# Another PSUM bank for one mask, an earlier load, and a reordered gate stage in a two-branch AdaLN block

## The chip, the cores and the metric

The kernel runs on one core of a Trainium2 chip, in one launch. The metric is device time in microseconds, the median of repeated runs. The engines are TensorE (PE), VectorE (DVE), ScalarE (ACT), GpSimd (POOL) and SyncE (SP), which issues nearly all of the DMAs.

## The reference

`x` has 2 batches of 512 rows of 512 features (`b`, `s`, `d`). A conditioning vector gives six modulation rows per batch. Two branches follow each other, each with a layernorm, a modulation and a gated residual:

```python
mod = (_silu(L0_c) @ L0_wmod).reshape(L0_c.shape[0], 6, 1, -1)
sa, ca, ga, sb, cb, gb = (mod[:, 0], mod[:, 1], mod[:, 2], mod[:, 3], mod[:, 4], mod[:, 5])
ga = (2 * (ga >= 0) - 1) * jnp.maximum(jnp.abs(ga), 0.25)   # gb alike
h = _layernorm(x, axis=-1) * (1 + ca) + sa
x = x + ga * _L0_attn_ref(h, mask, weight, bias)
h = _layernorm(x, axis=-1) * (1 + cb) + sb
x = x + gb * _L0_ffn_ref(h, w1, w3, w2, lora_A1, lora_B1, ...)
```

The first branch is one matmul with a 512 x 512 weight whose 32 x 32 blocks are kept where the sum of an integer mask over the block is above zero, plus a bias. The second is a gated feed-forward (512 to 1376 and back) with a rank-16 addition to each of its three weights. All is float32.

## The kernel before, in words

**Tiling.** Rows lie in eight tiles of 128 (batch 0: tiles 0 to 3, batch 1: 4 to 7; `b, t = divmod(n, T)`), features in `KT` = 4 groups of 128 (`k`). Float32 products are made of three float32r matmuls: each operand is split into a rounded high part and a low part (`ht_hi`/`ht_lo`, `wa_hi`/`wa_lo`), and high x high, high x low and low x high are summed in PSUM; these are `m` = 0, 1, 2 of `attend(b, k, m)` (L1093). Where the code has `b` in a modulation's index, it is the batch.

**Order.** Nothing plans the work. Each engine has one list of steps written by hand (SP from L357, POOL from L469, ACT from L622, DVE from L848, PE from L1175) and runs it in order; between engines there are only semaphores. So a step that waits holds up everything that stands behind it in its engine's list, also what is ready.

**The masked weight**, once per `k`: DVE's `mask_sum(k)` (L756) adds the mask in rows of 32; PE's `mask_blocks(k)` (L1073) adds over 32 partitions into a corner of `mask_bank(k)`, bank `side[0]` for k = 0, 1 and `acc[1]` for k = 2, 3 (for those it waits for `h_done(1)`, as `acc[1]` holds the second transposed group); DVE's `mask_on(k)` (L762) makes the flags and `mask_weight(k)` (L768, instruction L773) multiplies the weight in place; ACT's `masked_weight_high(k)` (L620) and POOL's `masked_weight_low(k)` (L467) split it.

**The normalised input**, once per batch: DVE's `moment(n)` (L699, L701), POOL's `root(n, 2)` for two tiles (L403, L406), DVE's `centres` (L717), then ACT's `norm` (L549) or DVE's `norm` (L710). PE's `turn(q)` (L978, L999) transposes one feature group of four tiles. Its banks are `acc[k]` for batch 0 and `acc[TURN_BANKS[k]]`, in the order 1, 0, 2, 3, for batch 1; q = 8 to 11 are the second branch's groups of batch 0. ACT's `high(q)` (L566) modulates and rounds, `whole(q)` (ACT L575 or DVE L736) modulates without rounding, and `low(q)` (POOL L419, some by DVE L725) is the difference. The first modulation's columns come from `mod_products` (L1026) and `first_columns`.

**The attention's accumulators.** Batch 0 sums in `front` = `up_a`, `up_b`, `side[0]`, `side[1]`, batch 1 in `acc`. `attend_bias(b)` (L1091) opens the four sums with the bias, one matmul for each, on four different groups of 32 rows.

**The gate.** `gate_rows(0)` (L1055) makes the raw gate, ACT's `gate_size(0)` its absolute value, DVE's `gates_of(0)` (L779, L782) the clamped gate in `gates_a`, and signals `gates_ready`. PE's `gate_spread` (L1068) broadcasts it over 128 partitions with eight float32 matmuls of 32 rows (16 records), two to each of the four `acc` banks, batch outside and bank inside, with one signal after the last; DVE's `gate_copy(q)` (L790) brings it to SBUF, once per bank, into the space of the mask. `turn(4 + k)` waits for copy k + 1. With the copies `attn_gate(n)` (L813) multiplies each attention tile, and `add_x1(n)` (DVE L818 for batch 0, POOL L437 for batch 1, by `X1_POOL`) adds it to `x`. The moments of the second branch follow.

**The rest.** `lora_high(n)` (ACT L616) and `lora_part(n)` (DVE L797) split the six pieces of the low-rank factors; POOL's `spread(j)` (L430) and PE's `merge(r)` (L1137, L1141) form their products, DVE's `merge` (L827) adds them to the weights streamed in from L378 on, `weight_low` (L833) makes `w_lo`. From about 53 us on PE works through `up` (L1156) and `down` (L1169 to L1171) for 2 x 11 hidden groups.

The DVE list from the last mask to the residual is the part that the change reorders most:

```python
            mask_on(3)
            mask_weight(3)
            moment(4)   # ... moment(5), moment(6), moment(7)
            centres(T)
            gates_of(0)
            norm(T + 2)
            norm(T + 3)
            for q in TURN_BANKS:
                gate_copy(q)
            lora_part(0)
            whole(4)    # ... whole(5), whole(6), whole(7)
            attn_gate(0)   # ... to attn_gate(3), then add_x1(0) to add_x1(3)
```

## Time and profile before

| | |
|---|---|
| median of 3 runs (lowest to highest) | 252.25 us (252.08 to 252.29) |
| the profiled execution: its own time, its span | 252.32 us, 250.5 us |
| PE busy | 242.3 us, 97% |
| DVE, ACT, POOL busy | 135.9, 89.6, 97.3 us |
| granted TensorE clock, mean | 1.000 |
| HBM read, written | 21.18 MB, 2.10 MB |

How to read it: the span runs from the first to the last instruction; the time is a little longer, by what lies around the program. A timeline row gives start, duration, engine, source line, operation, and how many instructions it joins. Where an instruction begins before the one ahead of it on the same engine has ended, the two overlap in the engine's pipeline. Idle time before an instruction and what released it stand in brackets.

### The profile page before, as it was taken

The numbers are of one execution on the slowest core, as the hardware profiler recorded it, in microseconds if no ns is written. First come the engines' busy times: TensorE is split into PE (matmuls) and PEld (weight loads), VectorE is DVE, ScalarE is ACT, GpSimd is POOL, SyncE is SP. The second block draws the span as 40 slices with busy tenths as digits, with TensorE's granted clock in tenths as the row PEclk, the third lists the DMA queues.
The fourth block names the chain that finished last, engine by engine and source line by source line (L and its number), as shares of the span: only waits on it lengthen the run. The fifth ranks groups of instructions, "written<-read, shape, count | busy, mean of one in ns | idle before, by whom it ended". The sixth has DMA issues, their size and how long they took to land.

```text
span 250.5 us, 3526 instructions
## 1 busy us (share of the span) xinstructions
PE 242.3 (97%) x1265; PEld 192.8 (77%) x1265; DVE 135.9 (54%) x221; ACT 89.6 (36%) x151; POOL 97.3 (39%) x102
## 2 busy tenths in 40 slices
PE   7799999899999999999999999999999999999993
PEld 6677768787788888888888778888888888888772
DVE  2847899899999744744754631741233123312224
ACT  2376554843324465465422311122112221222110
POOL 1377492326532131230210351497346435643300
PEclk9999999999999999999999999999999999999999
DMA  6999991023224413213217520030000000000005
GB/s 184 345 384 407 413 401 42 3 84 119 51 84 127 126 47 123 84 42 128 84 46 107 45 13 0 38 132 0 0 0 4 0 0 0 4 0 0 0 0 169
DMA packets 13041, 24.02 MB, mean 96 GB/s; under 512 B 1240, under 2 KB 2648, under 8 KB 13024
## 3 DMA queue, kind: packets, MB, share of 16 engines
q1 hardware_dynamic: 12864, 23.65, 30.2%
q8 instruction: 10, 0.16, 0.3%
q10 hardware_dynamic: 160, 0.15, 0.2%
q14 instruction: 7, 0.06, 0.1%
HBM read 21.18 MB, written 2.10 MB: 93 GB/s over the span
## 4 chain that ended last, share of the span: by engine, by line
PE 82%; DVE 6%; DMA 3%; issue 3%; POOL 2%; ACT 1%; SPq 1%; DVEq 0%; POOLq 0%; ACTq 0%
PE up_b L1156 25%; PE up_a L1156 24%; PE acc L1170 8%; PE acc L1171 8%; PE acc L1169 8%; DMA wmod_sb<-in_wmod 3%; PE side L1137 2%; DVE xt L839 1%; DVE stats L699 1%; PE acc L999 1%; DVE wa L813 1%; PE side L1141 1%; DVE xt L818 1%; PE acc L1106 1%; POOL ht_lo L419 1%
## 5 line engine op out<-in xcount | busy, mean ns | idle before, releaser
L940 DVE TENSOR_TENSOR g<-up_b,g 128x512 f32<-128x512 f32 (+1 forms) x22 | 15.2, 690 | 64.5 <-PE up_b L1156 64.5
L1170 PE MATMUL acc<-w_lo,g_hi 128*128 128x512 f32 (+1 forms) x88 | 34.7, 394 | 0.0
L1171 PE MATMUL acc<-w_hi,g_lo 128*128 128x512 f32 (+1 forms) x88 | 34.7, 394 | 0.0
L1169 PE MATMUL acc<-w_hi,g_hi 128*128 128x512 f32 (+1 forms) x88 | 34.6, 394 | 0.0
L670 ACT ACTIVATE g<-up_a 128x512 f32<-128x512 f32 (+1 forms) x22 | 13.1, 597 | 58.8 <-PE up_a L1156 58.5
L827 DVE SCALAR_TENSOR_TENSOR raw<-side,raw 128x512 f32<-128x512 f32 (+2 forms) x33 | 21.5, 676 | 22.3 <-PE side L1137 15.7
L677 ACT ACTIVATE g_hi<-g 128x512 fp32r<-128x512 f32 (+1 forms) x22 | 13.9, 633 | 49.4 <-DVE g L940 49.4
L462 POOL TENSOR_TENSOR w_lo<-work,w_hi 128x512 fp32r<-128x512 f32 (+1 forms) x11 | 14.2, 1287 | 41.1 <-ACT w_hi L604 41.1
L597 ACT ACTIVATE w_hi<-raw 128x512 fp32r<-128x512 f32 (+2 forms) x33 | 20.3, 626 | 21.2 <-DVE raw L827 21.1
L944 DVE TENSOR_TENSOR g_lo<-g,g_hi 128x512 fp32r<-128x512 f32 (+1 forms) x22 | 22.9, 1041 | 8.7 <-ACT g_hi L677 8.4
L1156 PE MATMUL up_a<-ht_hi,w_lo 128*128 128x512 f32 (+1 forms) x88 | 24.2, 396 | 0.4 <-DVE w_lo L833 0.4
L1156 PE MATMUL up_a<-ht_hi,w_hi 128*128 128x512 f32 (+1 forms) x88 | 24.3, 397 | 0.0
L833 DVE TENSOR_TENSOR w_lo<-raw,w_hi 128x512 fp32r<-128x512 f32 (+2 forms) x33 | 23.3, 736 | 1.6
L1156 PE MATMUL up_b<-ht_hi,w_lo 128*128 128x512 f32 (+1 forms) x88 | 24.1, 395 | 0.0
L1156 PE MATMUL up_b<-ht_hi,w_hi 128*128 128x512 f32 (+1 forms) x88 | 24.0, 394 | 0.0
L1156 PE MATMUL up_a<-ht_lo,w_hi 128*128 128x512 f32 (+1 forms) x88 | 24.0, 394 | 0.0
L1156 PE MATMUL up_b<-ht_lo,w_hi 128*128 128x512 f32 (+1 forms) x88 | 24.0, 394 | 0.0
L430 POOL TENSOR_SCALAR b<-parts,half_on 128x128 fp32r<-128x128 f32 (+1 forms) x22 | 14.2, 658 | 18.0 <-PE side L1137 15.0
L454 POOL TENSOR_TENSOR work<-w_hi,w_lo 128x512 f32<-128x512 f32 (+1 forms) x11 | 15.0, 1359 | 13.5 <-DMA work<-gates_f 12.1
L1156 PEld LDWEIGHTS up_a<-ht_hi,w_lo 128*128 128x128 f32 (+1 forms) x88 | 16.2, 186 | 5.0 <-DVE w_lo L833 0.9
L1171 PEld LDWEIGHTS acc<-w_hi,g_lo 128*128 128x128 f32 (+1 forms) x88 | 16.5, 188 | 3.9
L1156 PEld LDWEIGHTS up_a<-ht_lo,w_hi 128*128 128x128 f32 (+1 forms) x88 | 16.3, 185 | 4.2
(172 smaller groups left out, 379.3 us busy)
## 6 DMA issues: line engine op xcount, KB each, us to landing
raw<-in_ffn SPq DMA_DIRECT2D x33, 256.0 KB, 2.7
wmod_sb<-in_wmod SPq DMA_DIRECT2D x4, 1024.0 KB, 11.5
xt<-in_x SPq DMA_DIRECT2D x8, 256.0 KB, 8.2
wmod_sb<-in_wmod SPq DMA_DIRECT2D x1, 2048.0 KB, 15.1
out<-xt SPq DMA_DIRECT2D x8, 256.0 KB, 2.7
mask_sb<-in_mask SPq DMA_DIRECT2D x4, 256.0 KB, 9.2
wa<-in_weight SPq DMA_DIRECT2D x4, 256.0 KB, 9.2
lora_raw<-in_lora SPq DMA_DIRECT2D x1, 512.0 KB, 10.4
```

Source lines behind the costliest of these rows:

```text
L430: nc.gpsimd.tensor_scalar(b13[:, n, 0:w], f32(parts[:, LORA_B13 + j * P:LORA_B13 + j * P + w]), half_on[:, n:n + 1], None, ALU.mult).then_ ...
L454: nc.gpsimd.tensor_tensor(dst, f32(down_hi[j][0:w]), f32(down_lo[j][0:w]), ALU.add).then_inc(down_summed, 1)
L462: nc.gpsimd.tensor_tensor(down_lo[j][0:w], gated_sum[j % 2][0:w], f32(down_hi[j][0:w]), ALU.subtract).then_inc(gated_low_ready, 1)
L597: nc.scalar.activation(dst, src, ACT.Copy).then_inc(w_high_ready, 1)
L827: nc.vector.scalar_tensor_tensor(w, merge_bank(r)[0:rows, 0:cols], SCALING, w, ALU.mult, ALU.add).then_inc(merged, 1)
L833: nc.vector.tensor_tensor(low_part, src, f32(high), ALU.subtract).then_inc(w_ready, 1)
L940: nc.vector.tensor_tensor(g[0:w], up_b[0:w], g[0:w], ALU.mult).then_inc(g_ready, 1)
L944: nc.vector.tensor_tensor(g_lo[s % 2][0:w], g[0:w], f32(g_hi[s % 2][0:w]), ALU.subtract).then_inc(g_low_ready, 1)
L1156: last = nc.tensor.matmul(dst[0:w], w_part[j][:, k, n], h[b][:, k], start=(m == 0 and k == 0), stop=(m == 2 and k == KT - 1))
L1169: nc.tensor.matmul(acc[t][:], hi, down_hi[j][0:w], start=(j == 0), stop=False)
L1170: nc.tensor.matmul(acc[t][:], hi, down_lo[j][0:w], start=False, stop=False)
L1171: last = nc.tensor.matmul(acc[t][:], lo, down_hi[j][0:w], start=False, stop=(j == HT - 1))
```

## The change

It gives `mask_bank(1)` the bank `acc[3]`, so that `attend_bias(0)` can come ahead of `mask_blocks(1)` on PE, and moves `turn(3)`, `mask_blocks(2)` and `mask_blocks(3)` in PE's list. SP issues the four loads of batch 1's `x` ahead of the load of the gate's part of `wmod` (both 1 MB). `gate_spread` goes bank by bank and signals after each; two of the four copies go to ACT (a new semaphore `gate_row_by_act`); it runs after `attend(0, 3, 0)`. DVE and ACT make their norms of batch 1 ahead of `gates_of(0)` and `gate_size(0)`. POOL waits for `gates_ready` ahead of `low(3)` and `masked_weight_low(3)`, which swap places and come after two roots. `lora_part(1)` moves from behind `columns()` to just behind `lora_part(0)`, with `lora_high(1)` ahead of it on ACT. `add_x1(3)` goes to POOL, where it waits for three additions of DVE.

```diff
 
 WHOLE_DVE = (4, 5, 6, 7, 9, 11)
 
-X1_POOL = (4, 5, 6, 7)
+X1_POOL = (3, 4, 5, 6, 7)
 
 TURN_BANKS = (1, 0, 2, 3)
-GATE_COPIES = T
+GATE_COPIES = T // 2
 
 CENTRED = {0: 2, 1: 2, 4: 4, 5: 4, 8: 6, 9: 6, 10: 8}
 NORMS_ACT = (2, 4, 7)
...
         gates_ready = sem("gates_ready")
         spread_out = sem("spread_out")
         gate_row_ready = sem("gate_row_ready")
+        gate_row_by_act = sem("gate_row_by_act")
         gate_row_loaded = [sem(f"gate_row_loaded{b}") for b in range(B)]
         stats_ready = sem("stats_ready")
         moments_ready = sem("moments_ready")
...
             return acc[t] if b else front[t]
 
         def mask_bank(k):
-            return acc[1] if k >= 2 else side[0]
+            return (side[0], acc[3], acc[1], acc[1])[k]
 
         def mod_out_at(second, f):
             if second:
...
             load_first_mod(1)
             load_attention(2)
             load_attention(3)
+            load_x(1)
             load_mod(GATE_A, SHIFT_F, wmod_ga_loaded)
-            load_x(1)
             for n in range(LORA_FIRST):
                 load_lora(n)
             load_mod(SHIFT_F, GATE_F, wmod_f_loaded)
...
             def add_x1(n):
                 b, t = divmod(n, T)
                 pool.wait_ge(attn_gated, n + 1)
+                if n < T:
+
+                    pool.wait_ge(x1_by_dve, n)
                 nc.gpsimd.tensor_tensor(xt[:, b, t], mid[n % T], xt[:, b, t], ALU.add).then_inc(x1_by_pool, 1)
 
             def add_x2(n):
...
             low(1)
             masked_weight_low(2)
             low(2)
-            masked_weight_low(3)
-            low(3)
             root(T, 2)
             root(T + 2, 2)
+
+            pool.wait_ge(gates_ready, 1)
+            low(3)
+            masked_weight_low(3)
             spread(0)
             low(KT)
             low(KT + 1)
             low(KT + 2)
             low(KT + 3)
+            add_x1(T - 1)
             root(2 * T, 2)
             root(2 * T + 2, 2)
             spread(1)
...
                 nc.scalar.activation(gate_abs[:], gate_rows_out(n), ACT.Abs, scale=2.0
                                      ).then_inc(gate_abs_ready, 1)
 
+            def gate_copy(q):
+
+                act.wait_ge(spread_out, TURN_BANKS.index(q) + 1)
+                act.wait_ge(block_on_ready, KT)
+                src = acc[q][:, 2 * P:(2 + B) * P].rearrange("p (b n) -> p b n", b=B)
+                nc.scalar.activation(mask_sb[:, 0:B, q * P:(q + 1) * P].bitcast(F32), src, ACT.Copy
+                                     ).then_inc(gate_row_by_act, 1)
+
             def lora_high(n):
                 lo, hi = LORA_CUTS[n]
                 act.wait_ge(lora_loaded[n], 16)
...
             masked_weight_high(3)
             high(3)
             whole(3)
-            gate_size(0)
             norm(T)
             norm(T + 1)
+            gate_size(0)
             lora_high(0)
+            for q in TURN_BANKS[0::2]:
+                gate_copy(q)
+            lora_high(1)
             high(4)
             high(5)
             high(6)
             high(7)
-            for n in range(1, len(LORA_CUTS)):
+            for n in range(LORA_FIRST, len(LORA_CUTS)):
                 lora_high(n)
             mod_evacuate()
             norm(2 * T)
...
 
             def gate_copy(q):
 
-                dve.wait_ge(spread_out, 1)
+                dve.wait_ge(spread_out, TURN_BANKS.index(q) + 1)
                 dve.wait_ge(block_on_ready, KT)
                 src = acc[q][:, 2 * P:(2 + B) * P].rearrange("p (b n) -> p b n", b=B)
                 nc.vector.tensor_copy(mask_sb[:, 0:B, q * P:(q + 1) * P].bitcast(F32), src
...
                 b, t = divmod(n, T)
                 dve.wait_ge(attn_out, n + 1)
                 dve.wait_ge(gate_row_ready, GATE_COPIES)
+                dve.wait_ge(gate_row_by_act, GATE_COPIES)
                 if b:
 
                     dve.wait_ge(*x1_done(n - T))
...
             mask_weight(2)
             first_columns(1)
             mask_sum(3)
+            moment(4)
             mask_on(3)
             mask_weight(3)
-            moment(4)
             moment(5)
             moment(6)
             moment(7)
             centres(T)
-            gates_of(0)
             norm(T + 2)
             norm(T + 3)
-            for q in TURN_BANKS:
+            gates_of(0)
+            for q in TURN_BANKS[1::2]:
                 gate_copy(q)
             lora_part(0)
+            lora_part(1)
             whole(4)
             whole(5)
             whole(6)
...
             add_x1(0)
             add_x1(1)
             add_x1(2)
-            add_x1(3)
             moment(2 * T)
             moment(2 * T + 1)
             moment(2 * T + 2)
             moment(2 * T + 3)
             centres(2 * T)
             columns()
-            lora_part(1)
             centres(2 * T + 2)
             norm(2 * T + 3)
             gates_of(1)
...
                 pe.wait_ge(normed, NORMS_DVE[i])
                 if i == 1:
 
-                    pe.wait_ge(gate_row_ready, k + 1)
+                    pe.wait_ge(gate_row_ready if k % 2 else gate_row_by_act, k // 2 + 1)
                 elif i == 2 and k == 0:
 
                     pe.wait_ge(attn_gated, T)
...
                 pe.wait_ge(gates_ready, 1)
                 pe.wait_ge(cols_ready, 2)
                 pe.wait_ge(h_ready, KT)
-                for b in range(B):
-                    for q in range(KT):
-                        rows = slice(q * QUAD, (q + 1) * QUAD)
+                for q in TURN_BANKS:
+                    rows = slice(q * QUAD, (q + 1) * QUAD)
+                    for b in range(B):
                         row = q * QUAD + b
                         last = nc.tensor.matmul(acc[q][:, (2 + b) * P:(3 + b) * P],
                                                 ident[rows, row:row + 1].broadcast_to([QUAD, P]), gates_a[rows],
                                                 start=True, stop=True)
-                last.then_inc(spread_out, 1)
+                    last.then_inc(spread_out, 1)
 
             def mask_blocks(k):
                 blocks = slice(k * NB, (k + 1) * NB)
...
                 if b:
 
                     pe.wait_ge(gate_row_ready, GATE_COPIES)
+                    pe.wait_ge(gate_row_by_act, GATE_COPIES)
                 for t in ts:
                     if b:
                         pe.wait_ge(*h_done(KT + TURN_BANKS.index(t)))
...
             turn(1)
             turn(2)
             fill(FILL_H)
-            mask_blocks(1)
             pe.wait_ge(ones_ready, 1)
             pe.wait_ge(bias_ready, 1)
             pe.wait_ge(cols_ready, 1)
+            pe.wait_ge(block_on_ready, 1)
+            attend_bias(0)
+            mask_blocks(1)
+            attend(0, 0, 0)
             pe.wait_ge(block_on_ready, 2)
-            attend_bias(0)
-            attend(0, 0, 0)
+            turn(3)
             mod_products(0, 1)
-            turn(3)
+            attend(0, 0, 1)
             mask_blocks(2)
-            attend(0, 0, 1)
             first_columns(1)
             attend(0, 0, 2)
-            mask_blocks(3)
             attend(0, 1, 0)
             attend(0, 1, 1)
+            mask_blocks(3)
             attend(0, 1, 2)
             attend(0, 2, 0)
-            gate_rows(0)
             attend(0, 2, 1)
             attend(0, 2, 2)
+            gate_rows(0)
+            attend(0, 3, 0)
             gate_spread()
-            attend(0, 3, 0)
             turn(4)
             turn(5)
             turn(6)
```

## Rows read from the trace of the kernel before

**Rows 1.** The page: busy us, share, instructions by engine; GB/s in 40 slices

```profile
PE 242.3 (97%) x1265; PEld 192.8 (77%) x1265; DVE 135.9 (54%) x221; ACT 89.6 (36%) x151; POOL 97.3 (39%) x102
...
GB/s 184 345 384 407 413 401 42 3 84 119 51 84 127 126 47 123 84 42 128 84 46 107 45 13 0 38 132 0 0 0 4 0 0 0 4 0 0 0 0 169
```

**Rows 2.** Waits of PE: waiting, waited for, us in total, times, longest

```profile
PE up_a L1156 <- DVE w_lo L833: 0.4, 1, 0.4
```

**Rows 3.** Timeline, 14 to 18 us, all engines (start us, us)

```profile
14.41 0.29 PE L1080 MATMUL side<-mask_part,const 128*128 128x16 f32 x2
...
14.95 0.69 DVE L773 TENSOR_TENSOR wa<-wa,block_on 128x512 f32<-128x512 f32 x1
...
15.06 0.46 PE L1091 MATMUL up_a<-bias_parts,ones 32*128 32x512 f32 x1 [0.36 <-DVE block_on L765]
...
15.34 1.44 POOL L419 TENSOR_TENSOR ht_lo<-hbuf,ht_hi 128x512 fp32r<-128x512 f32 x1 [0.38 <-ACT hbuf L575]
...
17.01 0.78 ACT L575 ACTIVATE hbuf<-acc,shift,one_plus 128x512 f32<-128x512 f32 x1
```

**Rows 4.** Timeline, 16 to 21 us, all engines

```profile
16.62 1.08 PE L1026 MATMUL acc<-wmod_sb,silu_c 128*32 128x128 f32 x32
...
17.97 1.30 POOL L419 TENSOR_TENSOR ht_lo<-hbuf,ht_hi 128x512 fp32r<-128x512 f32 x1
...
18.67 1.15 DVE L773 TENSOR_TENSOR wa<-wa,block_on 128x512 f32<-128x512 f32 x1
...
19.85 0.63 PE L1106 MATMUL side<-wa_hi,ht_lo 128*128 128x512 f32 x2
...
20.85 0.48 PE L1106 MATMUL up_a<-wa_hi,ht_hi 128*128 128x512 f32 x1
```

**Rows 5.** Timeline, 23 to 30 us, all engines

```profile
23.36 0.69 DVE L699 BATCH_NORM_STATS2 stats<-xt 128x6 f32<-128x512 f32 x1 [0.98 <-DMA xt<-in_x]
...
26.51 0.18 DVE L701 BATCH_NORM_AGGREGATE moments<-stats 128x2 f32<-128x6 f32 x1
...
27.43 0.71 POOL L406 TENSOR_TENSOR rstd<-rstd,exponent 128x2 f32<-128x2 f32 x1
...
27.60 0.29 DVE L782 SCALAR_TENSOR_TENSOR gates_a<-gate_abs,gates_a 128x128 f32<-128x128 f32 x1
...
27.94 0.73 PE L1068 MATMUL acc<-gates_a,const 32*128 32x128 f32 x16
...
28.18 1.00 DVE L710 TENSOR_SCALAR work<-xt,moments,rstd 128x512 f32<-128x512 f32 x2 [0.30 <-POOL rstd L406]
...
29.66 1.94 PE L999 MATMUL acc<-const,work 128*128 128x128 f32 x16
```

**Rows 6.** Timeline, 29 to 34 us, DVE and PE

```profile
29.10 1.41 DVE L790 COPY mask_sb<-acc 128x256 f32<-128x256 f32 x4
...
31.14 1.53 DVE L736 TENSOR_SCALAR hbuf<-acc,one_plus,shift 128x512 f32<-128x512 f32 x2
...
33.40 0.54 PE L1091 MATMUL acc<-bias_parts,ones 32*128 32x512 f32 x3
```

**Rows 7.** Timeline, 34 to 46 us, all engines

```profile
34.03 0.68 DVE L813 TENSOR_TENSOR wa<-up_a,mask_sb 128x512 f32<-128x512 f32 x1
...
36.42 1.48 DVE L818 TENSOR_TENSOR xt<-wa,xt 128x512 f32<-128x512 f32 x1
...
37.82 1.88 DVE L818 TENSOR_TENSOR xt<-wa,xt 128x512 f32<-128x512 f32 x3
...
42.76 0.18 DVE L701 BATCH_NORM_AGGREGATE moments<-stats 128x2 f32<-128x6 f32 x1
...
43.07 0.74 DVE L797 SCALAR_TENSOR_TENSOR parts<-parts,const,lora_raw 128x512 fp32r<-128x512 f32 x1
...
43.11 0.78 POOL L403 TENSOR_SCALAR rstd<-moments 128x2 f32<-128x2 f32 x1 [0.52 <-DVE moments L701]
...
45.92 0.66 PE L999 MATMUL up_a<-const,work 128*128 128x128 f32 x4 [0.65 <-ACT work L549]
```

## The prediction

> **What bounds the kernel now.** I read the engine totals first: PE is busy for 242.3 of 250.5 us [rows 1], so from about 60 us on there is nothing but PE work, and the whole question is when that work begins. Then the list of PE's waits: one that the change can touch is an up product waiting 0.4 us for `w_lo` [rows 2]; two more stand in the timelines, 0.36 us of the first bias matmuls for the second mask's flags [rows 3] and 0.65 us before turn(8) [rows 7]. Together 1.4 us: that is all the PE idle time that a better order could win here, and any new PE wait counts against it in full. Then the timelines of DVE, ACT and POOL from 14 to 46 us, for who releases whom.
>
> One thing must be seen in them first. A DVE instruction with both inputs in SBUF and a POOL instruction of that kind don't run together: whichever starts second waits for the first. mask_weight(2) starts at 18.67 while POOL's low(1) runs from 17.97 to 19.27, and takes 1.15 us; it ends 0.55 after POOL [rows 4]. The same instruction at 14.95, ahead of POOL, takes 0.69, and there POOL's low(0), started at 15.34, takes 1.44: it ends 1.14 after DVE [rows 3]. The first add at 36.42 takes 1.48 while POOL is in low(7), and the next three together 1.88, 0.60 each from start to start; POOL's root at 43.11 takes 0.78 behind lora_part(1) at 43.07 [rows 7]. I call this the lock.
>
> **Step 1: bias ahead of the second mask.** The four bias matmuls (side by side, 0.46 us from 15.06) no longer wait for DVE's flags. They move in front of mask_blocks(1), which began at 14.41, so they start there (up to 0.1 later) and attend(0,0,0) starts at about 15.1 instead of 15.06 + 0.46 = 15.5: 0.4 gained. But the mask's sum is now behind them, at 14.85 to 14.95, and so are its flags and mask_weight(1): 14.95 + 0.44 to 0.54 = 15.39 to 15.50. POOL's low(0) depends on none of this and still starts at 15.34 [rows 3]. So POOL is now first, by 0.05 to 0.15 us, and the lock turns round: mask_weight(1) waits to 15.34 + 1.30 = 16.64 and ends at 16.64 + 0.55 = 17.19, not 15.64. That is 1.55 later, and ACT has its wa_hi, high and whole of k = 1 in a queue behind it: whole(1) ended at 17.01 + 0.78 = 17.79 [rows 3] and now ends at 19.34.
>
> **Step 2: what PE meets next.** attend(0,0,0) 1.1, turn(3) 0.5, mod_products 1.0 (16.62 began the latter before), attend(0,0,1) 1.0: PE is at mask_blocks(2) at about 18.76. It waits there for whole(1), as before, but that is at 19.4: 0.6 us idle. attend(0,1,0) then starts at about 20.7, against 20.85. Before, PE's matmuls of 19.85 were through at 20.3 and some 0.3 us was idle around mask_blocks(3) [rows 4], which now comes later and waits for nothing; that gain and the 0.4 of step 1 are nearly used up. mask_weight(2) and (3) each come 1.3 to 1.5 later than before (again partly behind the lock), mask_weight(3) ending at about 23.9.
>
> **Step 3: second x first.** DVE's first statistic of the second half waited for its x until 23.36 [rows 5]. One MB at the 401 to 413 GB/s of these slices [rows 1] is 2.6 us, so x is there at about 20.8 and the gate's weights, which have the same 1 MB, at about 25.3 instead. Neither is late: DVE is at its first moment at 22.0, PE at gate_rows(0) at 26.6. But three of the four moments are queued behind mask_weight(3). A moment is 0.82 (23.36 to 26.51 + 0.18 = 26.69 for four, with the last aggregate [rows 5]): 23.8 + 3 x 0.82 = 26.3, where they ended at 26.7. root(6) follows and ends at 27.55 (before 27.43 + 0.71 = 28.14 [rows 5]). Gained: 0.6 on the norms.
>
> **Step 4: the gates after the norms.** Before, gates_of(0) ran ahead of DVE's two norms and ended at 27.60 + 0.29 = 27.89, call that G. Now the norms (1.00) come first: 27.6 + 1.0 = 28.6, and gates_of 0.55 behind: G = 29.1, 1.2 later. PE has done attend(0,3,0) meanwhile (about 28.8) and waits 0.35 for the spread at 29.15. The spread ended 0.73 after its start [rows 5]. Its first copy can start 0.8 after G and takes 0.4, so turn(4) starts at G + 1.25 = 30.35: before 29.66. Sharing the copies saves two of four starts, 0.33 each [rows 6], off the last turn only, which does not wait for them.
>
> Here the order of the eight spread matmuls matters. Before, neighbours were in different groups of 32 rows, and the 16 records ended together after 0.73 us, which 16 one after another could not; now the four records of one bank share a group. The bounds: the same 0.7, or one record at a time at the 0.11 of the transposes (1.94 us for 16 [rows 5]), 1.9 us. I take the lower, since the next paragraph shows PE with over a microsecond to spare behind it. The Trainium skill ("TensorE: Matmul & The Clock Gate", Part 3, The mechanism) says that matmuls keep strict program order and overlap only across row groups; by that it would be the upper bound, turn(4) would start at G + 1.95, and the sum would not change as long as whole(6) is the later one.
>
> **Step 5: POOL held to the gates, and two lora parts.** low(3) and wa_lo(3) ran as soon as their inputs stood; they now wait for G. POOL starts 0.17 after its releaser (42.94 to 43.11 [rows 7]), so they run from G + 0.17 to G + 2.70 (1.3 each, the second begun a little before the first ends). DVE gets to lora_part(0) after its two copies, at G + 1.48, 0.07 behind the start of wa_lo(3): the lock again, to G + 2.70, and it ends at G + 3.2, where 0.6 alone would do (384 columns against the 0.74 for 512 of lora_part(1) [rows 7]). lora_part(1), moved here from 43.07, adds 0.67. whole(4) starts at G + 3.7. Before, the four started at 31.14 (G + 3.25) and gave way to attn_gate(0) at 34.03 [rows 7], so 0.72 each. PE's attend_bias(1) started at 33.40, when whole(6) ended (31.14 + 2 x 0.72 + 0.8) [rows 6]: G + 5.5 before, G + 5.95 now, 35.05, 1.65 later than before. PE itself is done with attend_last(0) at about G + 4.9, so 1.05 us idle, and even the serial spread (G + 5.55) fits below it.
>
> **Step 6: three adds.** attn_gate(0) starts at G + 6.6 (before G + 6.15). The add at G + 9.0 again finds POOL's low(7), which shifted along with spread(0) to end at G + 9.9; it ends at G + 10.45, then two more at 0.60, not three, and four moments of 0.81. The last moment ends at G + 14.9 = 44.0; before 42.76 + 0.18 = 42.94, G + 15.05 [rows 7]. POOL's add waits for the third DVE add and has 3.3 us for its 1.3: nothing, and only a root stands behind it, which waits for moments anyway. Without lora_part(1) the last root is not locked out and saves about 0.5: it was held from 43.11 to near 43.81, where lora_part(1) ended [rows 7]. ACT's norm(10) then ends at about 46.6, just ahead of PE: PE, 1.65 late with its own queue, is at turn(8) at 46.95. Before, 45.92 with 0.65 idle [rows 7]. So PE is 1.0 late there, the idle is gone. DVE is 0.8 late into its merges, so the 0.4 wait for `w_lo` [rows 2] shrinks to 0.2 and the end is 0.8 late.
>
> **Sum.** In PE's idle time up to attend_bias(1): new 0.6 (step 2), 0.35 and 0.55 (4), 1.05 (5) = 2.55; removed 0.36 before the bias, 0.3 around mask_blocks(3), and 0.25 in restarts after those waits, which I read off as the rest of the starts' difference: +1.65, as in step 5. After it 0.65 is removed before turn(8) and 0.2 of the `w_lo` wait: 1.65 - 0.85 = +0.8 us. The profiled execution took 252.32 us (span 250.5), the median is 0.07 less; 252.32 + 0.8 = 253.1.
>
> **Rivals.** A difference of 0.2% (0.5 us) is about what a measurement of this kernel can tell from no change.
> - *A, the forecast*, 253.1, chance 0.47. The chain of small leads may be wrong by 0.3 either way; low enough, it falls inside 0.5 us.
> - *B, DVE is first at the first lock.* If the flags come 0.1 earlier than I have them, mask_weight(1) starts before low(0) at 15.34. Then whole(1) ends at 18.2, PE does not wait at mask_blocks(2), and G is 28.3. Steps 5 and 6 still hold: attend_bias(1) at 34.25, turn(8) 0.2 late, end 0.2 late: 252.45. Against it: the lead of low(0) is worked out from starts; for it: it is only 0.05 to 0.15. Chance 0.25.
> - *C, faster.* G at 28.3 as in B, and DVE gets past the lora parts before POOL holds the lock, or is let in between low(3) and wa_lo(3): whole(4) at G + 2.95, since ACT's high(4) is ready at G + 2.9. Then attend_bias(1) is at 33.5, three adds and the free root bring norm(10) a whole microsecond earlier, turn(8) starts at 45.4 with no wait, and the `w_lo` wait shrinks too: 0.7 us faster, 251.55. It decides itself at whole(4): anything before G + 3.2 points here. For it: lora_part(0) misses by 0.07 only. Against: lora_part(1) must also wait for ACT's copies. Chance 0.22.
> - *D, the serial spread decides*: if the lock does not hold DVE but the spread takes 1.9, turns, high(4) to high(7) and attend_last come 0.65 later on top of A's late gates: 253.7. Chance 0.06.
>
> **Numbers.** Slower: D, and 0.44 of A's 0.47: 0.50. Within 0.2%: most of B and the rest: 0.27. Faster: C and a little of B: 0.23. The range runs from C to D with 0.1 either side: 251.5 to 253.8. The cases of both signs hold much of the chance; A's own range is 252.7 to 253.6.
>
> **What would show it.** In the changed profile: mask_weight(1) taking over 1.5 us with low(0) ahead of it (step 1; 0.7 means B); PE idle before mask_blocks(2) with ACT's hbuf as the releaser (2); gates_a finished at 29.1 (4); lora_part(0) over 1 us long and PE idle before the bias of the second half, released by DVE (5); three adds, the last root's first instruction well under 0.78 us, no PE wait before turn(8) (6). The forecast is wrong if gates_a is done by 28.3, or if attend_bias(1) starts before 33.9.

## The result, and the profile after

Interleaved with the kernel before on one chip, the changed kernel took 252.84 us (median of 7, 252.57 to 253.53), the one before 252.13 us (7 runs, 251.82 to 252.34): ratio 1.0031, 95% interval 1.0021 to 1.0040. That is slower by 0.3%, +0.71 us; the forecast was +0.8 (253.1 us).

The profiled execution took 253.53 us, the highest of its seven, so its span (251.7) is 1.2 us above before's; the other six spans are 250.7 to 251.2. 0.70 us of the 1.2 is there when the `w_lo` wait ends, at 61.26 us against 60.56, and still at the last matmul, at 246.93 against 246.23. The other 0.5 arises behind that, in the writing of the output. The medians differ by 0.71, so I don't count it as the change's, though no second trace shows it.

The page and PE's list of waits up to 66 us (waiting, waited for, us in total, times, longest):

```profile
PE 242.9 (96%) x1265; PEld 193.3 (77%) x1265; DVE 135.7 (54%) x218; ACT 90.0 (36%) x153; POOL 98.4 (39%) x103
```

```profile
PE acc L1196 <- DVE ht_lo L705: 1.4, 1, 1.4
PE up_b L1044 <- DMA wmod_sb<-in_wmod: 1.0, 1, 1.0
PE acc L1098 <- ACT hbuf L582: 0.5, 1, 0.5
PE acc L1017 <- ACT mask_sb L625: 0.5, 1, 0.5
PE up_a L1175 <- DVE w_lo L852: 0.4, 1, 0.4
PE acc L1086 <- DVE gates_a L800: 0.3, 1, 0.3
PE acc L1110 <- DVE g L754: 0.2, 1, 0.2
```

The first two rows (at 1.4 and 11.4 us) lie before the change's reach. Three of the next are waits that the forecast announced (0.6, 0.55, 0.35). The `w_lo` wait of [rows 2] is unchanged. The last row looks small and is not, as shown below.

Timeline of the changed kernel, 14 to 31 us, all engines (start us, us; the idle time before a group and its releaser stand in brackets):

```profile
14.46 0.50 PE L1110 MATMUL up_a<-bias_parts,ones 32*128 32x512 f32 x1
...
14.90 0.40 PE L1098 MATMUL acc<-mask_part,const 128*128 128x16 f32 x2
...
15.30 1.28 POOL L420 TENSOR_TENSOR ht_lo<-hbuf,ht_hi 128x512 fp32r<-128x512 f32 x1 [0.42 <-ACT hbuf L582]
15.33 0.17 DVE L783 TENSOR_SCALAR block_on<-acc 128x16 f32<-128x16 f32 x1 [1.27 <-PE acc L1098]
15.54 1.59 DVE L791 TENSOR_TENSOR wa<-wa,block_on 128x512 f32<-128x512 f32 x1
...
18.50 0.78 ACT L582 ACTIVATE hbuf<-acc,shift,one_plus 128x512 f32<-128x512 f32 x1
...
19.42 0.36 PE L1098 MATMUL acc<-mask_part,const 128*128 128x16 f32 x2 [0.53 <-ACT hbuf L582]
...
27.55 1.00 DVE L728 TENSOR_SCALAR work<-xt,moments,rstd 128x512 f32<-128x512 f32 x2 [1.21 <-POOL rstd L407]
...
28.79 0.29 DVE L800 SCALAR_TENSOR_TENSOR gates_a<-gate_abs,gates_a 128x128 f32<-128x128 f32 x1
...
29.14 0.75 PE L1086 MATMUL acc<-gates_a,const 32*128 32x128 f32 x16 [0.33 <-DVE gates_a L800]
...
30.41 1.94 PE L1017 MATMUL acc<-const,work 128*128 128x128 f32 x16 [0.52 <-ACT mask_sb L625]
```

The turned lock is in the third to fifth row: POOL at 15.30, mask_weight(1) at 15.54, 1.59 us long, where [rows 3] had DVE at 14.95 with 0.69. gates_a is done at 29.08 (before 27.89, [rows 5]); turn(4) starts 0.75 late.

The same view, 29 to 47 us:

```profile
30.38 1.29 POOL L471 TENSOR_TENSOR wa_lo<-wa,wa_hi 128x512 fp32r<-128x512 f32 x1
30.61 2.14 DVE L815 SCALAR_TENSOR_TENSOR parts<-parts,const,lora_raw 128x384 fp32r<-128x384 f32 x2
...
32.67 1.52 DVE L754 TENSOR_SCALAR hbuf<-acc,one_plus,shift 128x512 f32<-128x512 f32 x2
...
34.11 0.80 DVE L754 TENSOR_SCALAR g<-acc,one_plus,shift 128x512 f32<-128x512 f32 x1
34.13 0.61 PE L1110 MATMUL acc<-bias_parts,ones 32*128 32x512 f32 x2
...
34.97 0.50 PE L1110 MATMUL acc<-bias_parts,ones 32*128 32x512 f32 x1 [0.22 <-DVE g L754]
...
37.94 2.63 DVE L837 TENSOR_TENSOR xt<-wa,xt 128x512 f32<-128x512 f32 x3
...
40.72 1.29 POOL L441 TENSOR_TENSOR xt<-wa,xt 128x512 f32<-128x512 f32 x1 [1.90 <-DVE xt L837]
...
43.63 0.18 DVE L719 BATCH_NORM_AGGREGATE moments<-stats 128x2 f32<-128x6 f32 x1
...
43.98 0.23 POOL L404 TENSOR_SCALAR rstd<-moments 128x2 f32<-128x2 f32 x1 [0.52 <-DVE moments L719]
...
46.61 0.60 PE L1017 MATMUL up_a<-const,work 128*128 128x128 f32 x4
```

PE reaches the bias of the second half at 34.13, 3.7 us after turn(4), as in the kernel before (29.66 to 33.40, [rows 5, 6]). Two of the first three matmuls run; the third needs whole(6), which DVE ends at 34.11 + 0.80 = 34.91. Before, three ran side by side in 0.54 us. So PE shows 0.22 us idle there and loses 0.8: it is 0.73 late at the first of these matmuls and 1.52 late at the third (34.97 against 33.45). Before turn(8) it wins 0.83 back: the 0.65 wait of [rows 7] is gone and almost 0.2 of restarting with it (a matmul that need not wait starts before the one ahead of it has ended: turn(8) now starts 0.48 us behind the start of merge products that take 0.64). At 46.61 it is 0.69 late, and that is what reaches the end.

### The profile page after: what moved, and what is told of

Same layout as the page of the kernel before. It is cut to its first block, busy times and chain, and to the rows that moved or that the text cites. A ratio compares the mean times of both kernels' runs of the same rounds, so it can differ in the third digit from the quotient of the medians.

```text
span 251.7 us, 3531 instructions
## 1 busy us (share of the span) xinstructions
PE 242.9 (96%) x1265; PEld 193.3 (77%) x1265; DVE 135.7 (54%) x218; ACT 90.0 (36%) x153; POOL 98.4 (39%) x103
## 4 chain that ended last, share of the span: by engine, by line
PE 86%; DVE 5%; DMA 3%; issue 2%; SPq 1%; ACT 1%; POOL 0%; DVEq 0%; POOLq 0%
PE up_b L1175 24%; PE up_a L1175 24%; PE acc L1189 8%; PE acc L1188 8%; PE acc L1190 8%; PE acc L1125 4%; DMA wmod_sb<-in_wmod 3%; PE side L1156 2%; DVE xt L858 1%; PE side L1160 1%; DVE stats L717 1%; PE up_a L1044 1%; PE side L1024 1%; SPq L341 1%; DVE wa L791 1%
## 5 line engine op out<-in xcount | busy, mean ns | idle before, releaser
L1188 PEld LDWEIGHTS acc<-w_hi,g_hi 128*128 128x128 f32 (+1 forms) x88 | 16.5, 188 | 3.9
L1189 PEld LDWEIGHTS acc<-w_lo,g_hi 128*128 128x128 f32 (+1 forms) x88 | 16.5, 188 | 3.9
```

The costliest lines, as they stand in the source:

```text
L1188: nc.tensor.matmul(acc[t][:], hi, down_hi[j][0:w], start=(j == 0), stop=False)
L1189: nc.tensor.matmul(acc[t][:], hi, down_lo[j][0:w], start=False, stop=False)
```

## Experiments

Each kernel is the changed one with the edit shown (b3, b4, c1 and c2 have several), measured beside the kernel before. G is the end of gates_a. All times are from the kernel's own profiled execution, except the ratio. The first product of the modulation starts between 10.8 and 11.7 us in these executions; it waits for its weights' DMA in some of them (until 11.44 in the kernel before, 11.39 in the changed one) and for a mask in others (b4, a3), none of which the edits touch. So single times differ by some tenths for no reason of the edit, and the ratio decides.

| kernel | G | turn(4) | PE's arrival, turn(4) + 3.73 | whole(6) done | third bias | turn(8) | ratio (95%) |
|---|---|---|---|---|---|---|---|
| before | 27.89 | 29.66 | 33.40 | 33.39 | 33.45 | 45.92 | |
| after | 29.08 | 30.41 | 34.14 | 34.91 | 34.97 | 46.61 | 1.0031 (1.0021 to 1.0040) |
| a1 | 29.04 | 30.36 | 34.09 | 34.86 | 34.92 | 46.57 | 1.0031 (1.0020 to 1.0043) |
| a2 | 28.49 | 30.46 | 34.19 | 34.73 | 34.78 | 46.42 | 1.0022 (1.0013 to 1.0032) |
| a3 | 29.48 | 30.81 | 34.54 | 34.64 | 34.69 | 46.75 | 1.0013 (1.0004 to 1.0021) |
| a4 | 30.53 | 31.86 | 35.59 | 35.58 | 35.64 | 47.29 | 1.0099 (1.0074 to 1.0124) |
| b1 | 30.46 | 31.79 | 35.52 | 36.28 | 36.34 | 48.00 | 1.0096 (1.0083 to 1.0108) |
| b2 | 28.75 | 30.08 | 33.81 | 34.58 | 34.63 | 46.62 | 1.0032 (1.0020 to 1.0044) |
| b3 | 28.69 | 30.02 | 33.75 | 34.51 | 34.57 | 46.23 | 1.0027 (1.0011 to 1.0043) |
| b4 | 28.37 | 29.69 | 33.42 | 33.52 | 33.58 | 45.64 | 1.0001 (0.9990 to 1.0013) |
| c1 | 27.66 | 28.98 | 32.71 | 32.82 | 32.88 | 44.97 | 0.9979 (0.9969 to 0.9989) |
| c2 | 27.89 | 29.22 | 32.95 | 32.94 | 33.00 | 45.38 | 0.9978 (0.9967 to 0.9988) |
| c3 | 28.66 | 30.04 | 33.77 | 34.49 | 34.54 | 46.20 | 1.0020 (1.0011 to 1.0028) |

whole(6) done is whole(4)'s start + 2.24 (32.67 to 34.91 in the changed kernel). The third bias matmul starts 0.05 to 0.06 behind the later of the two columns to its left, in every kernel.

### a1: the second mask back ahead of the bias

```
-            attend_bias(0)
             mask_blocks(1)
+            attend_bias(0)
             attend(0, 0, 0)
```

> The changed kernel with mask_blocks(1) put back ahead of attend_bias(0) on PE; all else of the change stays. Lock theory: DVE's mask_weight(1) starts at 14.95, ahead of POOL's low(0) at 15.3, and takes 0.7 us and not 1.6; ACT's whole(1) ends at 17.8 and not 19.3; PE's 0.5 us wait before mask_blocks(2) is gone; gates_a is done at 28.2 to 28.4 instead of 29.1; the time falls by 0.4 to 0.6 us from the changed kernel, to about that of the kernel before. Rival (the early flags buy nothing, the gate stage is set by the late second x, the roots and its own order): gates_a stays within 0.2 us of 29.1 and the time within 0.2 us of the changed kernel's.

The first lock is undone, mask_weight(1) takes 0.69 us again from 14.72, and PE's wait ahead of mask_blocks(2) is gone. Nothing is won: ratio 1.0031, and PE waits 1.2 us for gates_a instead of 0.3. The lock has moved to the third mask (timeline of a1, 20 to 24 us):

```profile
21.96 1.29 POOL L420 TENSOR_TENSOR ht_lo<-hbuf,ht_hi 128x512 fp32r<-128x512 f32 x1 [0.24 <-ACT hbuf L582]
...
22.06 1.74 DVE L791 TENSOR_TENSOR wa<-wa,block_on 128x512 f32<-128x512 f32 x1
```

The three moments behind it end at 26.23 (26.27 in the changed kernel), and G is 29.04. The rival was right: of all the early loss (steps 1 and 2) nothing reaches the end, since G is set by DVE's list.

### a2: the gates back ahead of the norms

```
-            norm(T)
-            norm(T + 1)
             gate_size(0)
+            norm(T)
+            norm(T + 1)
...
-            norm(T + 2)
-            norm(T + 3)
             gates_of(0)
+            norm(T + 2)
+            norm(T + 3)
```

> The changed kernel with the gates back ahead of the norms of batch 1 on DVE and on ACT. Theory: gates_a is done at about 28.7 instead of 29.1, since gate_rows now comes late on PE anyway, but the norms then run into POOL's low(3) and low part of the weight, which start when the gates are ready, and whole(4), which sets PE's bias matmuls, stays within 0.4 us of 32.7: time within 0.3 us of the changed kernel's. Rival (the gates behind the norms are what costs the 0.7 us): whole(4) starts at or before 31.9 and the time falls by 0.5 us or more.

G is 0.6 earlier (0.4, counted from the first product of the modulation), but the norms now fall beside POOL's low(3), which gates_a releases. DVE in a2's timeline, and PE's wait (same columns as above):

```profile
28.41 1.95 DVE L728 TENSOR_SCALAR work<-xt,moments,rstd 128x512 f32<-128x512 f32 x2
```

```profile
PE acc L1017 <- DVE work L728: 1.2, 1, 1.2
```

turn(4) waits 1.2 us for the norms and starts no earlier. Ratio 1.0022, its interval overlaps the changed kernel's; the theory had asked for that, and the rival (0.5 us or more to win) fell.

### a3: lora_part(1) back to its old place

```
             lora_part(0)
-            lora_part(1)
             whole(4)
...
             columns()
+            lora_part(1)
```

(ACT's lora_high(1) also goes back behind high(7).)

> The changed kernel with lora_high(1) and lora_part(1) back at their old places. Theory (DVE's list in front of whole(4) sets PE): whole(4) starts about 0.6 us earlier (32.1), the second half's bias matmuls too, POOL's low(7) 0.4 earlier and with it the first add; but the last root is locked out again by 0.5 us, so that PE is ahead of it and waits some 0.2 us at turn(8): time 0.3 to 0.4 us below the changed kernel's. Rival (moving the lora part away from the root is what the change gains by): norm(10) is later, PE's wait of 0.65 us before turn(8) is back in full, time 0 to 0.4 us above the changed kernel's.

In this execution everything up to G came 0.4 later. From G on: whole(4) at G + 2.91 instead of G + 3.59, third bias 0.15 behind PE's arrival instead of 0.83; the last root is locked again and PE waits 0.24 us before turn(8). Ratio 1.0013 against 1.0031: the theory held, and about half of the loss was this one move.

### a4: POOL's wait for the gates dropped

```
-            pool.wait_ge(gates_ready, 1)
             low(3)
```

> The changed kernel without POOL's wait for the gates ahead of low(3); the order of its steps stays. Theory (the lock works for norms too): low(3) starts at 27.5 beside DVE's first norm, one of the norms takes 1.2 to 1.9 us instead of 0.55, gates_a is done 0.8 to 1.5 us later, lora_part(0) is no longer locked out; time 0.1 to 0.6 us above the changed kernel's. Rival (the wait itself costs, by pushing POOL's work behind the gates): norms stay at 0.55 us each, lora_part(0) takes 0.6 us, whole(4) starts 0.5 us earlier and the time falls by 0.4 us or more.

Timelines of a4, POOL, then DVE:

```profile
27.02 1.29 POOL L420 TENSOR_TENSOR ht_lo<-hbuf,ht_hi 128x512 fp32r<-128x512 f32 x1
28.28 1.44 POOL L471 TENSOR_TENSOR wa_lo<-wa,wa_hi 128x512 fp32r<-128x512 f32 x1
```

```profile
27.09 2.91 DVE L726 TENSOR_SCALAR work<-xt,moments,rstd 128x512 f32<-128x512 f32 x2 [1.21 <-POOL rstd L407]
```

The two norms start 0.07 behind low(3) and take 2.91 us instead of 1.00; G is 30.53, and PE waits 2.2 us for it. So the hold is what makes this order bearable. The six times are not one group, and the ratio of 1.0099 mixes them: 253.7 us in two (one of them the profiled one), 1.4 above the 252.28 of the kernel before, and 255.1 to 255.5 in four, whose mean granted clock was 0.989 to 0.993 against 0.999 to 1.000. The only other executions with a clock of 0.993 or less are two of nine of a1, one of five of b1 and one of ten of b3, each 0.6 to 1.7 us longer than its kernel's median, and all four kernels make PE wait 0.8 to 2.2 us for gates_a. That the wait brings the lower clock is not shown: b4 waits 1.0 us and has none among twelve, and none of those eight executions left a trace.

### b1: the second x back behind the gate's weights

```
-            load_x(1)
             load_mod(GATE_A, SHIFT_F, wmod_ga_loaded)
+            load_x(1)
```

> The changed kernel with the loads of batch 1's x back behind the gate's part of wmod. Theory (gates_a waits for norms, those for roots and moments, and these for the third mask and x): moment(4), which now stands ahead of mask_on(3), waits for its x until about 23.4, mask_weight(3) and the three moments behind it come 1.2 to 1.5 us later, gates_a is done at 30.3 to 30.6, time 1.0 to 1.4 us above the changed kernel's. Rival (the early load buys nothing, something else bounds the norms): time within 0.2 us of the changed kernel's.

The first moment of the second half waits for its x until 23.34, G is 30.46, PE waits 1.9 us for the gates, ratio 1.0096 (against 1.0031: 1.6 us more, where the theory had 1.0 to 1.4). With the norms ahead of the gates the early x is needed; it and the hold of a4 are the parts that cost most to undo.

### b2: the fourth add back on DVE

```
-X1_POOL = (3, 4, 5, 6, 7)
+X1_POOL = (4, 5, 6, 7)
...
+            add_x1(3)
             moment(2 * T)
```

(and POOL's add_x1(T - 1) taken out.)

> The changed kernel with the fourth addition back on DVE. Theory: the last moment comes 0.6 us later, and since norm(10) ends only 0.3 us before PE is ready for turn(8), PE waits 0.3 us there; DVE's merges come no later than PE's; time 0.2 to 0.6 us above the changed kernel's. Rival (PE is late anyway and covers the addition): time within 0.15 us of the changed kernel's.

```profile
37.61 3.22 DVE L836 TENSOR_TENSOR xt<-wa,xt 128x512 f32<-128x512 f32 x4
```

The list is 0.6 longer, as [rows 7] had it. PE waits 0.2 us before turn(8), where the changed kernel does not wait; the ratio, 1.0032, can't be told from the changed kernel's. So the rival's time held. In the trace turn(8) starts 16.54 us behind turn(4), in the changed kernel 16.20, and the end of the `w_lo` wait, counted the same way, lies 0.24 later, so the fourth add on POOL may win some 0.2 to 0.3 us, which these ratios, with intervals of 0.2%, don't show.

### b3 and b4: moments ahead of the fourth mask, then both

```
             moment(4)
+            moment(5)
+            moment(6)
             mask_on(3)
             mask_weight(3)
-            moment(5)
-            moment(6)
             moment(7)
```

> As a1_mask_first, with moments 5 and 6 also ahead of mask_on(3) on DVE. In a1 the third mask_weight was held by POOL's low(2) until 23.8 whatever its flags did, and the moments stood behind it. Theory (the moments behind that lock set the norms and the gates): mask_weight(3) still ends at about 23.8, the last moment ends at 25.4 instead of 26.2, gates_a at 28.2 to 28.4 instead of 29.0, and the time falls by 0.3 to 0.8 us from a1's. Rival (gates_a is bound by gate_rows on PE or by the norms on ACT): gates_a stays within 0.2 us of 29.0, time within 0.2 us of a1's.

> b3_moments_first with lora_part(1) and lora_high(1) back at their old places as in a3_lora_late. Theory (the late gates and DVE's list ahead of whole(4) are two separate costs, 0.75 and 0.8 us): whole(4) starts at about 31.2 as in the kernel before, the three additions then bring the last moment to 42.7 at the latest, and the time is 0.3 to 0.6 us below the kernel before (about 251.8). Rival (the two overlap, so that only one can be won back): the time stays at 252.2 or above.

b3 has a1's edit with it, b4 those of a1, b3 and a3. In b3 no mask_weight is locked (0.69 each) and the moments end at 25.15, over a microsecond earlier. G comes only 0.4 earlier, at 28.69, because gates_of now waits for ACT (DVE in b3's timeline):

```profile
26.42 1.00 DVE L728 TENSOR_SCALAR work<-xt,moments,rstd 128x512 f32<-128x512 f32 x2 [1.21 <-POOL rstd L407]
28.07 0.29 DVE L797 TENSOR_SCALAR gates_a<-acc 128x128 f32<-128x128 f32 x1 [0.65 <-ACT gate_abs L617]
```

whole(4) still follows G by 3.6, so the third bias waits as before: 1.0027. b4 takes that away too and runs at the time of the kernel before, 1.0001. The theory had asked for 0.3 more, the rival for no gain below the kernel before: the time is the rival's, 252.09 us against 252.16. The 0.65 us above, in which the gates wait for ACT, is still there in b4 (0.64); c1 takes it away.

### c1 and c2: the gate between ACT's norms, and lora_part(0) in a gap

c1 is b4 with

```
             norm(T)
-            norm(T + 1)
             gate_size(0)
+            norm(T + 1)
```

> Made of b4_moments_lora (which ran at the time of the kernel before), with one further edit: ScalarE's gate_size(0) stands between norm(T) and norm(T + 1) instead of behind both. In b4 gates_a waited 0.64 us for gate_abs (27.46 to 27.72) while VectorE had finished its two normalizations at 27.10. Theory (a chain over ScalarE, VectorE and PE sets the end of this stretch): gate_abs ends near 26.95, gates_a at about 27.75 instead of 28.37, turn(4) 0.5 to 0.6 earlier, and the kernel is 0.3 to 0.5 faster than before (ratio 0.998 to 0.999). Rival (VectorE's list from lora_part(0) to whole(7), locked by GpSimd, sets it): gates_a is early, but whole(4) and what follows keep their places relative to GpSimd's work, and the ratio stays at 1.000.

G is 27.66, PE no longer waits for the gates, and at the bias whole(6) is done only 0.1 us behind PE's arrival (c1's timeline, PE):

```profile
27.71 0.75 PE L1085 MATMUL acc<-gates_a,const 32*128 32x128 f32 x16
28.98 1.94 PE L1016 MATMUL acc<-const,work 128*128 128x128 f32 x16 [0.52 <-ACT mask_sb L625]
...
32.72 0.66 PE L1109 MATMUL acc<-bias_parts,ones 32*128 32x512 f32 x3
```

251.70 us against 252.14: 0.9979 (0.9969 to 0.9989), faster than both kernels, as the theory had it.

c2 also puts ACT's lora_high(0) ahead of norm(T + 1), lora_part(0) ahead of DVE's gate copies, and POOL's spread(0) behind low(7).

> As c1_gate_between, and besides: lora_high(0) also ahead of norm(T + 1) on ScalarE, lora_part(0) ahead of the two gate copies on VectorE (where it was idle 0.86 us in b4, waiting for the spread), and GpSimd's spread(0) behind low(7) instead of ahead of low(4) (its first reader, merge(0), starts near 45 us). Theory: lora_part(0) starts ahead of GpSimd's low(3), takes 0.7 us instead of 1.46, whole(4) starts near 30.3 instead of 31.29 in b4, low(4) of GpSimd 0.5 to 1.2 earlier, attend_bias(1) up to 1 us earlier, and the kernel is 0.7 to 1.2 us faster than before (ratio 0.995 to 0.997), unless something else comes last there: then x1's chain or the moments of batch 1 stay and the ratio is 0.998. Rival: lora_part(0) meets GpSimd's low(3) (which the gates release) and is locked behind it, delaying the gate copies and turn(4) by 0.6 or more: ratio 1.000 or above.

lora_part(0) takes 0.61 us from 27.80, ahead of POOL's low(3) at 27.97, which takes 1.58 instead of 1.27. whole(4) then waits for ACT (c2's timeline, DVE):

```profile
30.70 1.52 DVE L753 TENSOR_SCALAR hbuf<-acc,one_plus,shift 128x512 f32<-128x512 f32 x2 [1.02 <-ACT ht_hi L573]
```

DVE has a whole idle microsecond, and the ratio is 0.9978, as c1's. The rival fell, and of the theory only its exception stands (something else comes last, ratio 0.998): the lock was avoided and nothing came of it. ACT's high(4) holds whole(4), and PE reaches the bias at turn(4) + 3.73 whatever DVE does; in c1 DVE was only 0.1 behind that.

### c3: one signal, the old order of the spread

```
-                for q in TURN_BANKS:
-                    rows = slice(q * QUAD, (q + 1) * QUAD)
-                    for b in range(B):
+                for b in range(B):
+                    for q in range(KT):
+                        rows = slice(q * QUAD, (q + 1) * QUAD)
...
-                    last.then_inc(spread_out, 1)
+                last.then_inc(spread_out, 1)
```

(the copies wait for 1.)

> The kernel after with one part undone: the sixteen products of the spread in the order of before (for each batch the four row groups) and one signal behind the last, for which all four copies wait. In the trace of after the four signals came within 0.045 us of each other. Theory (matmuls of different row groups run side by side whichever order they stand in): nothing changes, ratio to the kernel before 1.003 as with after, spread about 0.73 to 0.75 us long, copies 0.05 us later at most. Rival (the order by bank with its own signals lets the first copy start early): the copies start 0.3 us or more later and the kernel is 0.2 to 0.3 us slower than after, ratio 1.004.

Spread at 28.72, first copies at 29.51, 0.79 behind its start; in the changed kernel ACT's first copy is 0.74 behind it and DVE's 0.80. Ratio 1.0020 (1.0011 to 1.0028), no slower than the changed kernel. Signalling by bank buys 0.05 us for one engine's first copy and nothing for the other's.

## Why the prediction was right

The direction, the size and most steps stood, each read off the rows above.

**Steps 1 and 2** happened as written: low(0) first, by 0.24 us, mask_weight(1) over at 17.13 (forecast 17.19), PE idle 0.53 (0.6). Rival B's condition, DVE first at that lock, did not hold.

But the sum counted this 0.6 as part of the +1.65, and a1 shows that to be the wrong account of what costs time: without it the time is the same. The forecast's own step 4 says why, had it been read on: G hangs on moments, roots and norms, and PE waits there for whatever it did not lose earlier. The same run refutes B's second half, that G would be 28.3 if the first lock went well. The next lock takes its place, with a lead of 0.10 us.

**Steps 3 and 4** were within 0.06: moments done 26.27 (26.3), G 29.08 (29.1), wait 0.33 (0.35), turn(4) 30.41 (30.35). The spread took 0.75: the lower bound was the measured one, and rival D's serial 1.94 fell. That was luck in part: the forecast took it because PE had time to spare, which says nothing of how the matmuls would run.

**Step 5.** whole(4) at G + 3.59 (G + 3.7), third bias at 34.97 (35.05). Its own terms, G + 3.2 and 0.67, add up to some G + 3.8 to 3.9; the end of the lock was 0.2 too late (in a3 lora_part(0) ends at G + 3.0), and the two slips nearly cancel. The forecast put the wait before the first bias matmul; it stands before the third, and PE's arrival is G + 5.05, not G + 4.9. a3 shows that the moved lora_part(1) makes 0.68 of the 0.83 that the third bias lies behind PE's arrival. Rival C's condition, whole(4) before G + 3.2, was not met. Meeting it is not enough: a4 does, at G + 2.80, and is slower, as its G is 30.53. b4 has both of C's conditions, G at 28.37 and whole(4) at G + 2.91, and takes the time of the kernel before, where C promised 0.7 less; with lora_part(1) in its old place the last root is locked again. Only c1 and c2, with G at 27.66 and 27.89, are faster than that kernel, by 0.5 us.

**Step 6.** Last moment 43.81 (44.0), the root's first instruction 0.23 us instead of 0.78 [rows 7], no wait before turn(8). Two errors cancel here. turn(8) is 0.69 late, not 1.0: 0.2 of short restarts and 0.1 of step 5 were not in the sum. And the `w_lo` wait did not shrink to 0.2; it is 0.4 to 0.5 us in every run. DVE's first merge, in the kernel before and in the changed one:

```profile
45.95 1.28 DVE L827 SCALAR_TENSOR_TENSOR raw<-side,raw 128x512 f32<-128x512 f32 x2
46.64 1.29 DVE L846 SCALAR_TENSOR_TENSOR raw<-side,raw 128x512 f32<-128x512 f32 x2 [0.28 <-PE side L1156]
```

Before, the merges and turn(8) (45.92) both came behind the last root. Now the root is early, and the merges wait for PE's merge products, which stand just ahead of turn(8) (46.61). Either way the merges start 0.03 us behind turn(8), in every kernel but b2 (0.07 ahead), and from there DVE's list runs without a wait to `w_lo`. So they are late by the same 0.69, and the wait between them stays.

The forecasts of A, 253.1, and of B and C, 252.45 and 251.55, start from different values of the kernel before, 252.32 and 252.25; nothing hangs on the 0.07.

So: +0.75 at turn(4) from the late gates, +0.8 more at the third bias from DVE's list, -0.8 before turn(8). The gates are late because the norms stand ahead of them (a2: 0.4 to 0.6) and the moments behind the fourth mask (b3: 0.3 to 0.4). The order of the norms is no loss in itself: c1 keeps DVE's norms ahead of the gates and has G at 27.66, since its moments are early and gate_size stands between ACT's norms. What remains, the early x (b1) and the hold (a4), pays for that order: without either it would be worse still.

## What to carry to other kernels

When an engine in order feeds another, write down when each list reaches their meeting point, and change only what comes last there; here the later of turn(4) + 3.73 and whole(6) sorts the kernels of the table, up to the tenths by which the executions differ anyway and but for a4, whose ratio mixes two groups of times. An idle time that lies ahead of a later wait for a third engine is no part of the sum: a1 removed 0.5 us of it for nothing. And a wait of 0.2 us can cost 0.8 when it breaks up matmuls that would have run side by side.

## What the runs showed of the hardware

**The lock of DVE and POOL holds the loser for whole instructions, and it does not need two inputs in SBUF on DVE's side.** The norms have one tensor input and two scalar columns. Beside POOL's subtractions two of them took 2.91 us (a4) and 1.95 (a2), alone 1.00; each norm that waits ends 0.28 us behind the POOL instruction it waits for (the locked mask_weight: 0.55), so in a4 each of the two waits for one. The prediction named only instructions with two SBUF inputs. (The Trainium skill, "SBUF — State Buffer", section "SBUF: two separate sides", names a second kind beside these, DVE operations in a two-port performance mode. That the norms are of that kind no row says; 0.5 us for one, against 0.69 for an operation with two SBUF inputs of that size, would fit.) A lead of 0.07 us (a4), 0.10 (a1) or 0.17 (c2, where DVE was first) decides who waits.

**Matmuls of different row groups run side by side even when neighbours in the program share one.** In the kernel before, neighbouring records of the spread were in different groups of 32 rows; in the changed one the four records of a group stand together. It still takes 0.75 us (before 0.73, [rows 5]), and its 16 records start in four batches of four, 0.01 to 0.02 us apart within a batch (29.14 to 29.18, then from 29.35, 29.46 and 29.57). The four records that carry the four signals, one of each bank, are the four of the last batch; the others bear no mark, and that each batch holds one of each bank is inferred from this. The Trainium skill ("TensorE: Matmul & The Clock Gate", Part 3, The mechanism) says that matmuls start and end strictly in program order. By that three of the four signals would have come batches earlier; the trace disagrees. (The 1.94 us that the prediction drew from it was too much: were only the last record of a bank to run beside the first of the next, 13 starts of 0.11 us would give 1.4, by estimate.)

**Four signals are not there at once.** The records that carry them end within 0.045 us of each other (29.840 to 29.885), but the semaphore's own events stand 0.059 us apart, at 29.855, 29.914, 29.973 and 30.032; with one signal (c3) its event comes 0.044 behind the last record's end, here the fourth comes 0.147 behind. ACT's first copy starts 0.02 behind the first event and DVE's 0.02 behind the second (timeline of the changed kernel):

```profile
29.88 0.66 ACT L625 ACTIVATE mask_sb<-acc 128x256 f32<-128x256 f32 x2 [1.41 <-PE acc L1086]
29.94 0.76 DVE L808 COPY mask_sb<-acc 128x256 f32<-128x256 f32 x2 [0.86 <-PE acc L1086]
```

That is why signals by bank bring nothing here: they win 0.05 us for the first reader and lose 0.1 for one that needs the last.
